# Opening pair of each layer in a four-layer modulated-convolution and FFN kernel: another order of the edge work, and an earlier load at the end of the FP8 stage

## The reference

```python
def _layer(x, style, w, b, mw, mb, typ):      # per sample weights
    s = style @ mw.T + mb
    weight = SCALE * w * s[:, None, :, None]
    weight = weight * rsqrt(sum(weight**2, axis=(2, 3)) + EPS)[:, :, None, None]
    if typ == 'same':         out = conv(x, weight) + b
    elif typ == 'upsample':   out = blur(conv_transpose2(x, weight) + b)
    elif typ == 'downsample': out = conv_stride2(blur(x), weight) + b
# the stack is: same, upsample, same, downsample
x = x + FFN0(stack0(x))    # FP8-quantised 1024x1024 product
x = x + FFN1(stack1(x))    # 1024x1024 product and top-2 of 16 LoRA experts
x = x + FFN2(stack2(x))    # 1024x1024 product and sparsemax of 8 LoRA experts
x = x + FFN3(stack3(x))    # low-rank gated FFN, 256 -> 2752 -> 256 -> 1024
```

## Time and profile before

| | us |
|---|---|
| median of 3 runs | 2149.49 (2143.9 to 2149.99) |
| the profiled execution's own time | 2145.14 |
| its span, first to last instruction | 2143.3 |
| PE busy | 2005.1 (94%) |
| DVE busy | 1145.0 (53%) |
| ACT busy | 915.5 (43%) |
| POOL busy | 380.2 (18%) |
| mean granted TensorE clock | 0.975 of 2.4 GHz |

### The profile page before, as it was taken

One profiled execution on the slowest core, in us unless ns is written; L12 is line 12 of the kernel. 1 busy time (PEld: TensorE's weight loads), 2 busy tenths in 40 slices (PEclk: granted clock), 3 DMA queues, 4 the chain that ended last, 5 costly groups with the idle time before them and its releaser, 6 DMA issues. The chain is left out here.

```text
span 2143.3 us, 30313 instructions
## 1 busy us (share of the span) xinstructions
PE 2005.1 (94%) x9870; PEld 1674.6 (78%) x9878; DVE 1145.0 (53%) x1971; ACT 915.5 (43%) x1393; POOL 380.2 (18%) x457
## 2 busy tenths in 40 slices
PE   4899968899999989998899999998999999999999
PEld 3677733789998978887788888877888878878886
DVE  5888888655545453325644444446555433343333
ACT  4477754444444431003433333324666544433442
POOL 4122211211111100102111111112212122222221
PEclk9899989999999999999999999998999999999999
DMA  7566646321111232224311111114333211132114
GB/s 179 180 186 182 176 152 231 133 78 59 59 59 68 69 128 79 78 98 139 102 59 59 59 59 59 59 50 130 102 105 100 89 47 51 44 134 93 51 44 161
DMA packets 100910, 213.75 MB, mean 100 GB/s; under 512 B 17280, under 2 KB 47488, under 8 KB 100096
## 3 DMA queue, kind: packets, MB, share of 16 engines
q1 hardware_dynamic: 99584, 211.18, 31.0%
q10 hardware_dynamic: 1280, 1.97, 0.4%
HBM read 150.65 MB, written 62.46 MB: 99 GB/s over the span
## 5 line engine op out<-in xcount | busy, mean ns | idle before, releaser
L999 PE MATMUL ps<-l_u_hi,l_g_hi 128*128 128x512 f32 x512 | 210.0, 410 | 17.6 <-DVE l_u_lo L1358 10.3
L1180 ACT ACTIVATE rows<-ps,l_EY,dem3e 128x512 f32<-128x512 f32 x128 | 99.2, 779 | 287.4 <-PE ps L999 270.3
L999 PE MATMUL ps<-l_u_lo,l_g_hi 128*128 128x512 f32 x512 | 205.7, 402 | 0.0
L999 PE MATMUL ps<-l_u_hi,l_g_lo 128*128 128x512 f32 x512 | 205.5, 401 | 0.0
L122 POOL TENSOR_TENSOR rows<-l_EY,ones 128x4 f32<-128x4 f32 x128 | 36.2, 283 | 806.3 <-ACT rows L1180 806.3
L2335 DVE SCALAR_TENSOR_TENSOR f_prod<-ps,b,f_gate 128x512 f32<-128x512 f32 (+1 forms) x88 | 66.0, 750 | 172.1 <-ACT f_gate L2275 172.1
L2376 POOL TENSOR_TENSOR x_lo<-f_prod,x_hi 128x512 fp32r<-128x512 f32 (+1 forms) x88 | 105.0, 1193 | 292.1 <-ACT x_hi L2282 292.1
L1358 DVE SCALAR_TENSOR_TENSOR l_u_lo<-ps,s_u,l_u_hi 128x512 fp32r<-128x512 f32 x128 | 95.1, 748 | 84.9 <-ACT l_u_hi L1162 84.8
L2205 PE MATMUL ps<-pt_hi,v_hi 128*128 128x512 f32 (+1 forms) x352 | 138.5, 394 | 1.7 <-PEq L590 1.7
L1162 ACT ACTIVATE l_u_hi<-ps,s_u 128x512 fp32r<-128x512 f32 x128 | 87.9, 689 | 121.3 <-PE ps L942 73.9
L2205 PE MATMUL ps<-pt_lo,v_hi 128*128 128x512 f32 (+1 forms) x352 | 138.5, 393 | 0.0
(11 more groups left out here) (341 smaller groups left out, 5027.8 us busy)
## 6 DMA issues: line engine op xcount, KB each, us to landing
x<-rows SPq DMA_DIRECT2D x64, 512.0 KB, 2.9
xin<-x SPq DMA_DIRECT2D x96, 256.0 KB, 4.0
rows<-x SPq DMA_DIRECT2D x48, 512.0 KB, 4.4
out<-rows SPq DMA_DIRECT2D x32, 512.0 KB, 2.6
v<-in_ffn_v SPq DMA_DIRECT2D x84, 128.0 KB, 2.6
xin<-in_x SPq DMA_DIRECT2D x16, 512.0 KB, 5.5
xb<-in_x SPq DMA_DIRECT2D x16, 512.0 KB, 3.3
x<-xb SPq DMA_DIRECT2D x16, 512.0 KB, 2.6
```

Of the source, the lines that this page charges most:

```text
L999: mm = nc.tensor.matmul(ps[:, 3 + h, :], Gs[ws][:, h, at:at + P], Us[ms][:, h, 1 + q:1 + q + HALF], start=(k == 0), stop=(k == 11))
L1180: nc.scalar.activation(hs[:, h, :], ps[:, 3 + h, :], ACT.Identity, bias=EY[:, 1, 0, bass.ds(h * NP + p, 1)], scale=dem3e[:, bass.ds(h * NP ...
```

## The change

The change reorders the first pair of every layer and one load at the end of the FP8 stage. No instruction of arithmetic is added or taken away.

```diff
+EDGE_BANKS = (7, 1)
             def edges_p():                       # PE
                 pe.wait_ge(ue_ready, n)
-                pe.wait_ge(g_summed, g0 + 1)
+                pe.wait_ge(ul_ready, 2 * g0 + 2)
...
-                                ps[:, 5 + h, 0:NP * 3 * PW].rearrange("p (n k) -> p n k", k=PW),
+                                ps[:, EDGE_BANKS[h], 0:NP * 3 * PW].rearrange("p (n k) -> p n k", k=PW),
             def edges_v():                       # PE
                 pe.wait_ge(pe_ready, n)
+                pe.wait_ge(g_summed, g0 + 1)
...
                 if first:                        # PE
+                    edges_p()
                     weights_a(1)
                     conv0_half(1, 0)
-                    edges_p()
                     main(0)
...
                 cross_g(1)                       # ACT, first_pair
-                if layer > 0:
-                    some_chunks(1)
-                else:
+                if layer == 0:
                     split_g(1)
...
             read_a(0)                            # DVE, opening
+            dve.wait_ge(zeros_ready, 2 * layer + 2)
+            edges_u()
             split_z(1)
             split_x_half(1, 0)
-            dve.wait_ge(zeros_ready, 2 * layer + 2)
-            edges_u()
-            some_maxima(1)
             sum_g(0)
+            split_g(0)
             split_x_half(1, 1)
-            split_g(0)
-            some_maxima(1)
+            some_maxima(2)
...
                 split_z(2)                       # DVE, first_pair
-                some_maxima(3)
-                if layer > 0:
-                    some_chunks(1)
+                some_maxima(2)
                 edges_v()
                 read_u(1, 0)
                 read_u(1, 1)
                 edges_y()
-                some_chunks(2)
+                some_chunks(3)
                 some_maxima(KB)
...
                 sum_g(1)
...
-                some_chunks(1)
                 split_h(0)
...
+            if layer > 0:                        # POOL, ahead of the bias copy and the chunks
+                pool.wait_ge(ue_ready, n)
...
             sp.wait_ge(sem("l0_xb_stored"), 16 * NP)     # SP, FP8 stage
-            with sp.Fori(0, NP // 2 - 1) as j:
+            for s in range(2):
+                store(s, s)
+                load(s + 2, s)
+            sp.wait_ge(stored[0], 16)
+            load_planes(sp, K.xin, sem("x_loaded"), x_dst, 0)
+            with sp.Fori(1, NP // 2 - 1) as j:
...
-            sp.wait_ge(stored[0], 8 * (NP - 2))
-            load_planes(sp, K.xin, sem("x_loaded"), x_dst, 0)
```

More of the change, by code:

```diff
@@ L1420, in edges_p @@
                         f4 = f.rearrange("p (n s) k -> p n s k", s=3)
-                        src = ps[rows, 5 + h, 0:NP * 3 * PW].rearrange("p (n s k) -> p n s k", s=3, k=PW)
+                        src = ps[rows, EDGE_BANKS[h], 0:NP * 3 * PW].rearrange("p (n s k) -> p n s k", s=3, k=PW)
                         step(v.tensor_tensor(f4, src, outer2(a2e[rows, own], 3, PW), ALU.mult))
```

## The result

The changed kernel took 2136.77 us (median of 5, 2135.28 to 2138.69), the kernel before 2149.49 beside it: a ratio of 0.9948 on record, 95% interval 0.9937 to 0.9958, so 11 us faster by that ratio, which takes in every execution and not the middle ones alone; the two medians lie 12.7 us apart. Forecast were 2140.7 us and a range of 2131 to 2148.5.

What follows compares the result with a forecast made beforehand. PE, busy 94%, was taken as the bound, except in openings, set by DVE reaching `edges_p` and `edges_v`. Terms -5.3 + 0.9 + 0.1 - 1.8 - 0.3 = -6.4 us, from a mean of 2147.1 to 2140.7; range 2131 to 2148.5.

Steps and rivals of the forecast that it cites:

- FP8 stage, -5.3: End of the FP8 stage: with x loaded early, layer 1's first convolution starts without a pause, at full rate; -5.3 us.
- Layer 0, +0.9: Layer 0's opening: DVE idles for ACT's split of G, and a fourth maximum delays `sum_g(1)`; +0.9 us.
- Layer 1, +0.1: Layer 1's opening: POOL and DVE exclude each other on SBUF, `edges_v` +1.2, `ffn(0)` 1.1 earlier; +0.1 us.
- Layers 2 and 3, -1.8 and -0.3: Openings: layer 2 gains -0.7 at `edges_v` and 1.1 at `ffn(0)`, layer 3 an earlier main(0); -1.8 and -0.3 us.
- The 10.6 us of PE's wait are no measure of the gain: All four openings: priced by when DVE reaches `edges_p` and `edges_v`, not by PE's removed 10.6 us wait for G's sum.
- rival 3: Openings: PE waits twice ahead of main(0) and falls to the lower clock; slower, +5.6 us, 2153; chance 0.08.
- Rival 1: Openings: POOL and DVE collide less, so gains follow PE's removed wait; 2135 us, 2130 at full ends; chance 0.20.
- Rival 2: Layer 1 starts 5.3 us earlier but waits for a DMA or the last store; price 5.3, 2146 us; chance 0.14.

Runs made afterwards that it cites:

- e1: The kernel before with only the early load of layer 1's x, all openings as they were: 2145.32 us, ratio 0.9981.
- before 2: Second profile of the kernel before, unchanged, run again beside the changed kernel on one chip: 2145.79 us.
- e4: The changed kernel with POOL's bias copies and lo parts of weight chunks turned into zero fills that read no SBUF: 2132.70 us, ratio 0.9925.
- e5: The changed kernel with `cross_g` ahead of ACT's first chunk in the opening: 2139.88 us, ratio 0.9958.
- e8: The changed kernel with only PE's edge product put back behind its second convolution half: 2145.54 us, ratio 0.9982.
- r3: The kernel of e8 unchanged, run again beside the changed kernel on one chip: 2144.61 us, ratio 0.9982.
- e7: The changed kernel with e5's edit and three maxima in place of two ahead of `edges_v` in layer 0: 2138.80 us, ratio 0.9954.
- r2: The changed kernel unchanged, run again beside the kernel before on one chip: 2136.61 us, ratio 0.9957.

## Why the prediction was right, and where it was not

The time fell into the range and on the forecast side, but the sum had one true large term and left out another.

- **FP8 stage, -5.3.** Right: -5.5 in e1, and the earlier trace rows to L191 at 361.85 shows the mechanism. All of the step's conditions (no idle time of ACT, DVE's residual add ahead of the split, the full rate behind it) are in the rows. Alone it was worth 4 us of time, and where the rest of the 5.5 went is not shown.
- **Layer 0, +0.9.** Measured: main(1) 0.7 us earlier from the start of the span, but 0.8 later behind `read_a`. The new idle time for ACT and the fourth maximum are there (`read_a` to `edges_p` 11.1 us instead of 10.1, `edges_y` to `sum_g(1)` 5.3 instead of 4.2), but `read_a` itself began 1.5 us earlier. The first convolution's 12 matmuls took 4.3 us instead of 5.3, and 4.2 to 5.3 in the other profiles, with the old order and with the new, so I take that for the execution's and not the edit's. Two more profiles with the old order (before 2 and load only) have main(1) 0.3 to 0.6 us later behind `read_a` than after, so the loss itself is no larger than the scatter.
- **Layer 1, +0.1.** Measured +2.0 against the first profile, +0.2 and -0.2 against the second. `edges_p` came 17.4 us behind the layer's start, against 14.8 and 16.2 in the two profiles of before: +2.7 or +1.2, forecast +2.1. The chain of POOL and DVE was priced well, and e4 confirms its cause. What was missing, cross_g behind a chunk that waits for its DMA, costs the opening 0.6 to 1.1 us at most, since POOL's chunks fill most of that time (e5).
- **Layers 2 and 3, -1.8 and -0.3.** Measured -2.3 and -1.4 against the first profile of before, -1.4 and -1.4 against the second. (By its own terms the sum of layer 2 is -1.9: 1016.8 is 0.8 under 1017.61, not 0.7.)
- **"The 10.6 us of PE's wait are no measure of the gain"** is the sentence that failed. It is true of DVE's chain, as e8's profile shows, and waits as such were not saved (13.0 us of new ones for 10.6). But it valued PE's order at nothing, while that order decides how much of the work runs at the lower clock. The term is what e8 and r3 lack: by medians 6 to 7 us beside e5 to e7 and 8 beside after, by ratios 5.4 beside after, as large as the largest of the sum or larger. I had the mechanism in hand as rival 3 and put it on the wrong side. It takes the kernel before, whose PE waits ahead of the edge product, below full clock in main(0) in all six openings of layers 1 to 3 in its two profiles, and in load only's three with the same order; with the edge product early 22 of 27 openings in nine profiles have 1.00 there. Before, layers 1 to 3:

```profile
385.43:392.49 7.06, 7.06 (x27) 5.63 (x27) 6.39 (x15) 1.16 (x3) 1.08 (x1) 0.81 0.24 77
1007.58:1015.76 8.18, 8.16 (x26) 6.53 (x26) 7.48 (x22) 0.69 (x1) 0.00 (x0) 0.69 0.17 59
1466.06:1473.74 7.68, 7.68 (x27) 6.13 (x26) 7.08 (x18) 0.69 (x1) 0.00 (x0) 0.74 0.60 160
```

The new order is no guarantee: in layer 2 after itself has 0.64, with main(0) taking 8.7 us instead of 5.9. And with the edge product late and the rest new, four of six openings have 1.00 (e8, r3), so main(0) alone does not account for the 5 to 8 us either. That the place of the product costs them is measured; that it does so through the clock is seen in r3's layer 3 and in the granted clocks of the executions (medians of 0.974 to 0.977 late, 0.978 to 0.981 early in after, r2 and e5 to e7), and its way to the stages far behind is not shown.

- **Rival 1** gave 2135 to 2130 and is near in time by luck: no collision went away, and `edges_p` starts later in layer 1 and no earlier in layer 2 (17.9 us behind the layer's start, before 17.7). **Rival 2** is wrong at its price of 5.3. Layer 1's first chunk does land 7.5 us behind the layer's start where it had landed after 5.4, and by e5 that costs the opening 1.1 us at most.

The rows don't add up to the whole. How the lower level comes to lie longer over work far behind the openings (the join ahead of the gated FFN, from the last `ffn`, takes 8.2 us at its longest and 5.8 at its shortest, with no edit near it) is open; it goes with the kernel but also with the execution, and no run here separates them.

## What to carry to other kernels

A wait of TensorE that looks free, because another engine's chain sets the end, still has a price if TensorE then runs at 1.2 GHz for the work behind it: fill the pause with any product whose inputs are ready. Take the medians of ten or so executions for it, since here the same kernel had executions of 2137 and of 2147 us, and a single profile of it showed no loss at all. Price an opening twice, by the chain of waits and by the granted clock of the windows, and take a second profile of the old kernel before believing differences of 1 to 2 us. Where a VectorE instruction with both inputs in SBUF meets a GpSimd instruction that reads SBUF, count each at its full time for both engines (0.74 us became 2.89 here), and give it to the engine that does it in half.

## What was not expected of the hardware

- Half or more of the gain (5.4 us by the ratios, 8.0 by the medians, of 11 and 12.7) hangs on the place of one product on TensorE, and goes with its clock. TensorE was at its lower level for 106 to 110 us in four of five profiles with the edge product late (the fifth, e8's, had 83.1), and for 76 to 93 in all nine with it early.
- 10 us taken out of three openings (e4) made 4 to 7 us of time: its profile was at the lower level for 93.0 us, after's for 82.8. Shorter openings do not always mean a shorter time at the lower level.
- The first matmuls behind a pause of 13.16 us go in steps of 0.43 us, at 1.2 GHz by that step. The trace's record of the granted clock begins only at 50.48 us, where the step falls, so the 1.00 that a window ahead of it shows is no reading. In all 14 profiles the record begins where this step falls, or within 0.5 us of it, at 50.0 to 53.6 us. PE in layer 0 of after, where the step falls from 0.42 to 0.25:

```profile
47.30 0.79 PE L944 MATMUL ps<-x_hi,c_hi 128*128 128x512 f32 x1 [13.16 <-POOL l_u_lo L1660]
...
50.03 0.60 PE L944 MATMUL ps<-x_hi,c_hi 128*128 128x512 f32 x1
50.45 0.41 PE L944 MATMUL ps<-x_lo,c_hi 128*128 128x512 f32 x1
50.70 0.40 PE L944 MATMUL ps<-x_hi,c_lo 128*128 128x512 f32 x1
```
